# A fused language-model block: in SyncE's list of DMA work of a step, the two stack loads are moved to the end

## Chip, cores, metric

One core of one Trainium2 chip. The metric is the device time of one execution in microseconds (us), median of several runs. The program is given each engine's instructions in a fixed order, written out by hand; engines meet at semaphores alone.

## What is computed

For 32 sequences of 512 tokens, width 128: an embedding of position, nesting depth and segment times a matrix; attention with 8 heads of 16 channels on its layernorm; and a gated mixture of 4 low-rank experts on the layernorm of that. Each adds to its input.

```python
h = tok(x, pos_table, nest_table, seg_table, W)                     # [32, 512, 128]
h = h + attn(layernorm(h), qkv_w, qkv_b, out_w, out_b)
h = h + ffn(layernorm(h), gate_w, thr_w, fc1_w, lora_A, lora_B, fc2_w)

# attn: 8 heads of c = 16
scores = einsum('bshc,bthc->bhst', q, k) / sqrt(c)
ctx = einsum('bhst,bthc->bshc', softmax(scores), v)
out = ctx @ out_w.T + out_b

# ffn: weights = relu(softmax(xf @ gate_w.T) - sigmoid(xf @ thr_w.T) / 4), made to sum to 1
lo = relu(xf @ fc1_w[e].T) @ lora_A[e] @ lora_B[e] @ fc2_w[e].T     # for each expert e
out = sum over e of weights[:, e] * lo
```

## The kernel before

The work is a software pipeline over sequences. Step t (t = -4 to 34) does parts of up to nine sequences at once: it embeds sequence t + 4, makes q, k and v of t + 3, the row maxima of t + 2 and t + 1, the softmax products of t, and projection and experts of t - 2 and t - 3. A step has 16 slots. In each slot TensorE (PE) runs two tiles of scores for row maxima (L642, "mix<-kstk,qstk"), two tiles of the scores that go into the exponential (L621, "sc<-qstk,kstk"), one product of another part, and in every second slot the product with the values (L632, "pv"). VectorE (DVE) takes the row maxima (L876), ScalarE (ACT) the exponentials (L504).

Queries and keys are split in three bf16 pieces each. The pieces are stored to DRAM ("stack_dram<-pieces", L308, six DMAs a sequence) and loaded back, replicated and rearranged, as 96 partitions of `qstk` and `kstk` (three DMAs each, L315 and L322; 1.5 MB a sequence). These are the stack loads, `("stack", 3, 0)` and `("stack", 3, 1)`: in step t they are those of sequence t + 3, and four buffers of them exist. The first reader is L642 of that sequence, in slot 8 of step t + 1.

The softmax subtracts the row maximum inside the matmul: 24 further partitions of `qstk` hold the maxima of each row, turned by PE (product "mT", slot 12), copied by ACT into `mT` (L531) and spread by one DMA of 192 KB, `("max_in", 1, 0)`, "qstk<-mT" (L338). In step t it is that of sequence t + 1, and the first L621 of step t + 1 waits for it (`s_mrow`). Half 0 of sequence t's denominators is stored just ahead of it (`("den_out", 0, 0)`, L328, after ACT's copy of slot 12); behind it the gate weights of sequence t - 2 are stored (`weights_out`, L334, after ACT's copy of slot 12) and loaded back as rows (`weights_in`, "wrow<-w_dram", L366), which first waits until the store has landed. `weights_in` is read by DVE (L950) in slot 3 of the next step.

All these DMAs are issued by SyncE (SP) on one queue, in the order of the list `SP_WORK`: each entry is a kind of work, the sequence relative to t, and a part. SP runs the list once a step; where an entry waits, all behind it wait. Behind the list's end stands the next step's beginning: the token rows ("ids_b", needed by DVE in slot 9), the first piece (which waits for ACT's piece, and for the q stack of the sequence before it to have landed, since the DRAM buffer is single: `upto(sp, s_stk[side], b - 1, 48)`), half 1 of the denominators (`den_out`, L328), two more pieces, and the load of the denominators (`den_in`, L344, after both halves have landed), which DVE inverts in slot 7 (L895).

Of the kernel before, what the change touches and what calls it, by code (L numbers as in the profile page):

```python
# [76 lines left out]
SP_WORK = [  # L77
    ("ids", 4, 0), ("piece", 3, (0, 0)), ("den_out", -1, 1), ("piece", 3, (0, 1)), ("piece", 3, (0, 2)),
    ("den_in", -1, 0), ("piece", 3, (1, 0)), ("piece", 3, (1, 1)), ("out", -3, 0), ("piece", 3, (1, 2)),
    ("rden_out", -1, 0), ("rden_in", -1, 0), ("stack", 3, 0), ("stack", 3, 1), ("den_out", 0, 0), ("max_in", 1, 0),  # L80
    ("weights_out", -2, 0), ("weights_in", -2, 0),
]

EPS = 1e-5
# [962 lines left out]
```

## Time and profile before

| | |
|---|---|
| median of 3 runs | 1260.97 us (1260.73 to 1262.85) |
| the profiled execution | 1249.84 us, span of its instructions 1248.0 us |
| PE busy | 1140.1 us, 91% of the span |
| DVE, ACT, GpSimd (POOL) busy | 908.2, 821.6, 592.6 us |
| mean granted clock of PE | 0.963 of full speed |
| moved by DMA | 123.98 MB, 99 GB/s over the span |

The busy time of PE is modelled at its ends: a matmul of 512 columns is shown 0.38 us long, but the next may start 0.22 us after it. Full steps run from about 190 to 1116 us of the span; ahead of them the pipeline fills, behind them it drains.

### The profile page before, as it was taken

The page shows a single profiled execution, that of the slowest core. Times are in us where ns is not written, and L with a number is a line of the kernel's source. Part 1 is how long each engine was busy: PE and PEld are TensorE (multiplying, and loading weights), DVE is VectorE, ACT ScalarE, POOL GpSimd, SP SyncE. Part 2 cuts the span into 40 slices and gives each one's busy share as a digit, 9 for nine tenths or more (in the row PEclk, how much of TensorE's full clock was granted, in tenths as well). Part 3 has the DMA queues.
Part 4 walks back from the last instruction along what each step waited for, and adds up shares of the span by engine and source line. Part 5 has one row for each costly group of instructions (what it writes and reads, how often), then busy time and mean ns, then how long its engine had stood idle before and what let it go on. Part 6 is the DMA issues. An engine that isn't in the chain of part 4 may idle for free.

```text
span 1248.0 us, 20409 instructions
## 1 busy us (share of the span) xinstructions
PE 1140.1 (91%) x6392; PEld 447.1 (36%) x6392; DVE 908.2 (73%) x2370; ACT 821.6 (66%) x1602; POOL 592.6 (47%) x588
## 2 busy tenths in 40 slices
PE   3579799999999999999999999999999999999985
PEld 1223333333333333333434333333333333333332
DVE  6387687777787877777778777777788777778422
ACT  0217677777777766767777777767777777677851
POOL 2643454455445545544455445544554555432222
PEclk7669999999999999999999999999999999999988
DMA  3654444344455543445544434445544444451111
GB/s 81 140 103 87 104 98 101 92 102 102 111 117 114 114 99 95 100 95 113 121 110 113 99 94 106 103 109 117 113 116 104 99 92 108 102 114 43 44 62 35
DMA packets 88377, 123.98 MB, mean 99 GB/s; under 512 B 17469, under 2 KB 69054, under 8 KB 82054
## 3 DMA queue, kind: packets, MB, share of 16 engines
q1 hardware_dynamic: 86720, 121.08, 42.8%
q10 hardware_dynamic: 1550, 1.59, 0.5%
q8 instruction: 52, 0.85, 0.3%
q14 instruction: 55, 0.45, 0.1%
HBM read 80.81 MB, written 34.95 MB: 93 GB/s over the span
## 4 chain that ended last, share of the span: by engine, by line
PE 65%; DMA 23%; DVE 5%; ACT 2%; issue 2%; POOL 2%; SPq 0%; POOLq 0%; ACTq 0%; DVEq 0%
DMA qstk<-mT 20%; PE pv L632 15%; PE mix L642 14%; PE sc L621 14%; PE mix L659 4%; PE mix L664 3%; PE mix L654 3%; PE mix L694 2%; PE mix L710 2%; PE mix L677 2%; DVE negmax L876 2%; PE mix L699 2%; ACT mT L531 1%; PE mix L684 1%; DMA wrow<-w_dram 1%
## 5 line engine op out<-in xcount | busy, mean ns | idle before, releaser
L876 DVE TENSOR_REDUCE negmax<-mix 128x1 f32<-128x512 f32 x1024 | 672.9, 682 | 176.6 <-PE mix L642 172.4
L504 ACT ACTIVATE probs<-sc 128x512 f32<-128x512 f32 x1024 | 583.7, 598 | 239.6 <-PE sc L621 235.4
L621 PE MATMUL sc<-qstk,kstk 120*128 120x512 bf16 x1024 | 383.6, 384 | 39.1 <-DMA qstk<-mT 38.5
L642 PE MATMUL mix<-kstk,qstk 96*128 96x512 bf16 x1024 | 355.8, 390 | 11.2 <-DVE negmax L876 5.6
L632 PE MATMUL pv<-probs,vals 128*32 128x512 f32 x2048 | 272.7, 604 | 0.0
L457 POOL TENSOR_TENSOR ctxh<-ctx_sb,rdenb 128x512 f32<-128x512 f32 x64 | 81.3, 1270 | 304.0 <-DMA rdenb<-rden_dram 303.8
L642 PEld LDWEIGHTS mix<-kstk,qstk 96*128 96x128 bf16 x1024 | 99.8, 98 | 334.2 <-DVE negmax L876 198.0
L621 PEld LDWEIGHTS sc<-qstk,kstk 120*128 120x128 bf16 x1024 | 99.2, 97 | 175.8 <-issue 57.2
L694 PE MATMUL mix<-xn2T,fc1T_sb 128*128 128x512 f32 x256 | 134.5, 609 | 0.0
L413 POOL TENSOR_TENSOR hb_sb<-h_sb,obias 128x512 f32<-128x512 f32 x32 | 40.7, 1271 | 140.9 <-DVE h L901 140.9
L562 ACT ACTIVATE hid<-mix 128x512 f32<-128x512 f32 x128 | 76.5, 598 | 26.9 <-PE mix L694 26.9
L424 POOL TENSOR_TENSOR pieces<-qk,pieces 128x512 bf16<-128x512 f32 x64 | 74.2, 1160 | 36.5 <-ACT pieces L519 36.4
L901 DVE TENSOR_TENSOR h<-mix,hb_sb 128x512 f32<-128x512 f32 x32 | 22.1, 692 | 85.2 <-PE mix L677 85.2
L441 POOL TENSOR_TENSOR pieces<-qkr,pieces 128x512 bf16<-128x512 f32 x64 | 74.0, 1157 | 8.5
L632 PEld LDWEIGHTS pv<-probs,vals 128*32 128x32 f32 x2048 | 40.4, 108 | 102.7 <-issue 75.8
L418 POOL TENSOR_TENSOR qkr<-qk,pieces 128x512 f32<-128x512 f32 x64 | 74.1, 1158 | 0.0
L406 POOL TENSOR_TENSOR ve<-mv,eps_sb 128x4 f32<-128x4 f32 x64 | 13.0, 203 | 126.8 <-DVE mv L872 126.8
L659 PE MATMUL mix<-xnT,qkvT_sb 128*128 128x512 f32 x128 | 70.4, 636 | 1.6 <-ACT xnT L509 1.4
L408 POOL TENSOR_TENSOR rstd<-ve,minus_half 128x4 f32<-128x4 f32 x64 | 65.2, 1019 | 5.0
L654 PE MATMUL mix<-id,xn 128*128 128x128 f32 x256 | 41.8, 289 | 23.4 <-POOL xn L450 15.2
L537 ACT COPY ctx_sb<-pv 128x512 f32<-128x512 f32 x64 | 37.6, 588 | 36.0 <-PE pv L632 36.0
L694 PEld LDWEIGHTS mix<-xn2T,fc1T_sb 128*128 128x128 f32 x256 | 49.6, 196 | 21.9 <-issue 4.6
(116 smaller groups left out, 1066.9 us busy)
## 6 DMA issues: line engine op xcount, KB each, us to landing
stack_dram<-pieces SPq DMA_DIRECT2D x192, 128.0 KB
rdenb<-rden_dram SPq DMA_DIRECT2D x64, 256.0 KB
qstk<-stack_dram SPq DMA_DIRECT2D x32, 384.0 KB, 6.4
kstk<-stack_dram SPq DMA_DIRECT2D x32, 384.0 KB, 8.7
qstk<-stack_dram SPq DMA_DIRECT2D x32, 256.0 KB, 6.8
kstk<-stack_dram SPq DMA_DIRECT2D x32, 256.0 KB, 9.4
wrow<-w_dram SPq DMA_DIRECT2D x32, 256.0 KB
out<-out_sb SPq DMA_DIRECT2D x32, 256.0 KB, 2.3
```

Of the source, the lines that this page charges most:

```text
L418: pool.tensor_tensor(qkr[:, side, :], qk32[:, side, :], pieces[:, side, 0, :], ALU.subtract).then_inc(s_res0, 1)
L424: pool.tensor_tensor(pieces[:, side, 1, :], qk32[:, side, :], pieces[:, side, 0, :], ALU.subtract).then_inc(s_pc1, 1)
L457: pool.tensor_tensor(ctxh[:, g, :], ctx_sb[:, u % 2, g, :], rdenb[:, g, :], ALU.mult).then_inc(s_ctxh, 1)
L504: act.activation(probs[:, c % 8, i % 2], sc[:, i % RING], ACT.Exp).then_inc(s_exp, 1)
L562: act.activation(hid[:, e, :], aux(f"fc1_{e}", 1), ACT.Relu).then_inc(s_hid, 1)
L621: pe.matmul(sc[:, i % RING, :], kstk[0:KROWS, u, h, j * P:(j + 1) * P], qstk[0:KROWS, u, h, :], start=True, stop=True).then_inc(s_score, 1)
L632: mm = pe.matmul(pv[Q * i:Q * i + Q, :], vals[:, u, 2 * half + jj, 4 * g + i, :], probs[:, 4 * (r % 2) + i, jj, :], start=(half == 0 and j ...
L642: pe.matmul(max_bank(m), qstk[0:STK, u, h, j * P:(j + 1) * P], kstk[0:STK, u, h, :], start=True, stop=True).then_inc(s_mxmm, 1)
L654: mm = pe.transpose(aux(name)[:, j, :], src[:, j, :], id32[:])
L659: pe.matmul(aux("qk"[side], 1), qkvT_sb[:, side, :], xnT[:], start=True, stop=True).then_inc((s_qmm, s_kmm)[side], 1)
L694: pe.matmul(aux(f"fc1_{e}", 1), fc1T_sb[:, e, :], xn2T[:], start=True, stop=True).then_inc(s_fc1mm, 1)
L876: dve.tensor_reduce(negmax[:, m // NT, m % NT:m % NT + 1], max_bank(m), AX.X, ALU.max, negate=True).then_inc(s_max, 1)
```

## The change

```diff
@@ -77,8 +77,8 @@
 SP_WORK = [
     ("ids", 4, 0), ("piece", 3, (0, 0)), ("den_out", -1, 1), ("piece", 3, (0, 1)), ("piece", 3, (0, 2)),
     ("den_in", -1, 0), ("piece", 3, (1, 0)), ("piece", 3, (1, 1)), ("out", -3, 0), ("piece", 3, (1, 2)),
-    ("rden_out", -1, 0), ("rden_in", -1, 0), ("stack", 3, 0), ("stack", 3, 1), ("den_out", 0, 0), ("max_in", 1, 0),
-    ("weights_out", -2, 0), ("weights_in", -2, 0),
+    ("rden_out", -1, 0), ("rden_in", -1, 0), ("den_out", 0, 0), ("max_in", 1, 0), ("weights_out", -2, 0),
+    ("weights_in", -2, 0), ("stack", 3, 0), ("stack", 3, 1),
 ]
```

No other engine's order changes, and no instruction is added or taken away. In SP's order, this is a full step from the load of the inverted denominators ("rdenb") to the next step's first piece, before:

```order
L359 DMA rdenb<-rden_dram 128x1x512 x2
L315 DMA qstk<-stack_dram 48x1x4096
L315 DMA qstk<-stack_dram 32x1x4096
L315 DMA qstk<-stack_dram 16x4096
L322 DMA kstk<-stack_dram 48x4096
L322 DMA kstk<-stack_dram 32x1x4096
L322 DMA kstk<-stack_dram 16x4096
L328 DMA den_dram<-ctx_sb 4x512
L338 DMA qstk<-mT 24x8x512
L334 DMA w_dram<-wT 4x4x128
L366 DMA wrow<-w_dram 128x1x512
L301 DMA ids_b<-ids_dram 64x512
```

The same place in the changed kernel:

```order
L359 DMA rdenb<-rden_dram 128x1x512 x2
L328 DMA den_dram<-ctx_sb 4x512
L338 DMA qstk<-mT 24x8x512
L334 DMA w_dram<-wT 4x4x128
L366 DMA wrow<-w_dram 128x1x512
L315 DMA qstk<-stack_dram 48x1x4096
L315 DMA qstk<-stack_dram 32x1x4096
L315 DMA qstk<-stack_dram 16x4096
L322 DMA kstk<-stack_dram 48x4096
L322 DMA kstk<-stack_dram 32x1x4096
L322 DMA kstk<-stack_dram 16x4096
L301 DMA ids_b<-ids_dram 64x512
```

The six stack loads have moved past four DMAs and past the waits of three of them: for ACT's copies of slot 12 and for the landing of the weights' store. They now stand directly ahead of the next step's token rows.

## Rows read from the trace of the kernel before

**Rows 1.** The page's shares, by line, of the chain that ended last

```profile
DMA qstk<-mT 20%; PE pv L632 15%; PE mix L642 14%; PE sc L621 14%; PE mix L659 4%; PE mix L664 3%; PE mix L654 3%; PE mix L694 2%; PE mix L710 2%; PE mix L677 2%; DVE negmax L876 2%; PE mix L699 2%; ACT mT L531 1%; PE mix L684 1%; DMA wrow<-w_dram 1%
```

**Rows 2.** Waits of the whole span: who for whom, us, times, longest

```profile
PE sc L621 <- DMA qstk<-mT: 38.5, 30, 5.5
...
PE mix L642 <- DVE negmax L876: 5.6, 11, 1.4
```

**Rows 3.** PE in time: start, us, line, [idle before <- releaser]

```profile
578.61 0.39 PE L642 MATMUL mix<-kstk,qstk 96*128 96x512 bf16 x1
578.84 0.38 PE L621 MATMUL sc<-qstk,kstk 120*128 120x512 bf16 x1
...
583.17 0.39 PE L642 MATMUL mix<-kstk,qstk 96*128 96x512 bf16 x1
584.68 0.39 PE L621 MATMUL sc<-qstk,kstk 120*128 120x512 bf16 x1 [1.12 <-DMA qstk<-mT]
...
601.90 0.39 PE L642 MATMUL mix<-kstk,qstk 96*128 96x512 bf16 x1
```

**Rows 4.** PE in time, the first L621 of three other full steps

```profile
439.65 0.39 PE L621 MATMUL sc<-qstk,kstk 120*128 120x512 bf16 x1 [2.51 <-DMA qstk<-mT]
...
475.56 0.39 PE L621 MATMUL sc<-qstk,kstk 120*128 120x512 bf16 x1 [1.53 <-DMA qstk<-mT]
...
619.46 0.39 PE L621 MATMUL sc<-qstk,kstk 120*128 120x512 bf16 x1 [0.40 <-DMA qstk<-mT]
```

**Rows 5.** PE in time, first L621 of two steps, 0.61 us instead of 0.39

```profile
153.58 0.61 PE L621 MATMUL sc<-qstk,kstk 120*128 120x512 bf16 x1 [5.51 <-DMA qstk<-mT]
...
547.80 0.61 PE L621 MATMUL sc<-qstk,kstk 120*128 120x512 bf16 x1 [2.37 <-DMA qstk<-mT]
```

**Rows 6.** Stretches: us, busy of PE, PEld, DVE, ACT, POOL; clock, DMA share, GB/s

```profile
153.50:159.50 6.00, 5.92 (x27) 3.73 (x27) 3.40 (x10) 2.88 (x5) 1.27 (x1) 0.61 0.00 0
547.50:552.50 5.00, 4.70 (x23) 3.23 (x27) 2.25 (x5) 2.32 (x5) 1.27 (x1) 0.68 0.22 72
```

**Rows 7.** SP's issues in time, one full step: start, us of issuing, DMAs

```profile
569.86 1.85 SPq L315 DMA_DIRECT2D qstk<-stack_dram  x3
571.80 1.57 SPq L322 DMA_DIRECT2D kstk<-stack_dram  x3
...
576.18 0.89 SPq L338 DMA_DIRECT2D qstk<-mT  x1
577.17 0.63 SPq L334 DMA_DIRECT2D w_dram<-wT  x1
584.87 0.55 SPq L366 DMA_DIRECT2D wrow<-w_dram  x1
...
591.51 0.62 SPq L308 DMA_DIRECT2D stack_dram<-pieces  x1
594.19 0.53 SPq L328 DMA_DIRECT2D den_dram<-ctx_sb  x1
...
597.37 0.40 SPq L344 DMA_DIRECT2D den<-den_dram  x1
```

**Rows 8.** SP's issues in time in a step of the draining end

```profile
1139.91 0.84 SPq L338 DMA_DIRECT2D qstk<-mT  x1
1140.85 0.64 SPq L334 DMA_DIRECT2D w_dram<-wT  x1
1143.56 0.54 SPq L366 DMA_DIRECT2D wrow<-w_dram  x1
```

**Rows 9.** Stretches of that step: us; clock, DMA share, GB/s

```profile
1141.00:1143.50 2.50, 1.00 0.39 92
1143.50:1144.50 1.00, 1.00 0.00 0
```

**Rows 10.** DMA issues: KB each, median us from issue to landing

```profile
qstk<-stack_dram SPq DMA_DIRECT2D x32, 128.0 KB, 8.5
kstk<-stack_dram SPq DMA_DIRECT2D x32, 128.0 KB, 10.8
```

**Rows 11.** DVE in time, same step as rows 7

```profile
601.05 0.34 DVE L895 RECIPROCAL rden<-den 128x32 f32<-128x32 f32 x1
```

**Rows 12.** The loads of the denominators, min/median/max of issue to landing

```profile
DMA to landing us min/median/max: 1.6/2.1/3.1
```

## The prediction

> **What bounds the kernel now.** I read the chain of waits first. The reader is to see that one DMA, the spreading of the turned maxima, is 20% of the chain that ended last, and that everything else of size in it is PE's own matmuls [rows 1]. The list of waits gives the same from PE's side: the first L621 of a step waits for that DMA, 38.5 us in 30 steps, while PE lost only 5.6 us to VectorE's row maxima, most of it while the pipeline fills [rows 2]. PE in time shows where it stands: L642 starts at 583.17, and the L621 behind it only at 584.68, with 1.12 us of idle time before it [rows 3].
>
> Is PE the bound outside this wait? Compare the distance between first L621s with the wait in it. From 439.65 to 475.56 it is 35.91 us, with 1.53 us idle at its end; from 584.68 to 619.46 it is 34.78 us with 0.40 us idle [rows 3, 4]. To the idle time I add 0.16 us, since it is counted from the modelled end of L642 (583.17 + 0.39), while an L621 behind L642 otherwise starts 0.23 us after its start (578.61 and 578.84) [rows 3]: the step truly lost 584.68 - 583.17 - 0.23 = 1.28 us, not 1.12. Then both distances without their waits are 34.22 us. A long wait gives the other engines nothing that makes the rest of the step shorter, and a short one takes nothing from them. So no other engine stands close behind, and a step without the wait should take 34.22 us.
>
> **Why the maxima come late.** SP issues the six stack loads at 569.86 to 573.4, then, when ACT has copied, the maxima at 576.18 and the weights' store at 577.17 [rows 7]. The last part of the k stack lands a median 10.8 us after its issue [rows 10], so at about 572.8 + 10.8 = 583.6. The maxima, behind them on the same queue, let PE go at 584.68, 8.5 us after their issue. The end of the program shows the same DMA with no stack load ahead of it, since there no sequence t + 3 exists: issued at 1139.91, and the core's DMA engines are empty from 1143.5 on [rows 8, 9], so at most 3.6 us. That tail is this change's steady state for this DMA, seen in the kernel before.
>
> By the Trainium skill (DMA: Bandwidth & Descriptors, Queues, rings and completion order) descriptors on each DMA engine are consumed in ring order. The trace agrees: 8.5 us behind the stacks against at most 3.6 us without them. The page's fit for a single DMA (Anatomy of one DMA, for the GpSimd path), 2.0 us + bytes / 436e3, would give 192 KB an estimated 2.5 us; either value clears the need below, so the sum is the same by both.
>
> **The change, part by part.** *Maxima:* issued at 576.18 as before (ACT's copy ends then, and SP was already free), landed by 576.18 + 3.6 = 579.8. PE wants them at 583.17 + 0.23 = 583.4. Cover 3.6 us, so the wait goes whole, also where the maxima were longest under way. Saved: 38.5 us, and 30 x 0.16 = 4.8 us of hidden ends; 43.3 us.
>
> *Clock:* behind two of the waits, 5.51 and 2.37 us long, PE ran at half its clock (1.2 instead of 2.4 GHz): the L621 there takes 0.61 us [rows 5]. Granted clock 0.61 over 6.0 us costs (1 - 0.61) x 6.0 = 2.3 us, and 0.68 over 5.0 us costs 1.6 us, of which 0.2 us lies in the wait itself [rows 6]; I take 2.3 + 1.4 = 3.7 us. The wait of 2.51 us at 439.65 had no such cost [rows 4]. Without the waits the two should be gone.
>
> *Weights' store and rows:* at the end of the program the rows' load follows its store by 2.7 us, in a full step now by 7.7 us [rows 7, 8]. So it is issued at about 579.9, five us earlier than now, and nobody waits for it: gain and cost nothing.
>
> *Stack loads:* they follow the rows' load, at 580.4 to 584.0. SP stood idle in just that time, waiting for the weights' store, and the token rows behind them were issued at 585.4 anyway: no entry of the next step is issued later. What is late is the landing. By [rows 10], counted from the issue of each: last q part 581.7 + 8.5 = 590.2, last k part 583.5 + 10.8 = 594.3. These durations had 512 KB of "rdenb" ahead of them and the maxima beside them; now 256 KB of weights' rows, so they are rather an upper bound; the lower bound is some 9 us from 580.4, 589.5.
>
> Who needs them, in a timeline in which the next step begins 1.3 us sooner? (a) The first L642 of that sequence, 601.90 - 1.3 = 600.6 [rows 3]: 6.3 us of cover against 18 now. (b) The next first piece, 591.51 - 1.3 = 590.2 [rows 7], waits for the q stack: cover nothing or 0.5 us. Were it 1 us late, SP would still be free ahead of the denominators' store at 594.19 - 1.3 = 592.9. (c) That store and the pieces are now queued behind the end of the k stack; this is the narrow place. The load of the denominators is due at 597.37 - 1.3 = 596.1 and lands 2.1 us later [rows 7, 12], at 598.2; VectorE inverts at 601.05 - 1.3 = 599.8 [rows 11]. With a stack that lands at 594.3, the store behind it lands at about 595, ahead of 596.1. Cost nothing; cover 1.1 us there and 1.6 us behind it.
>
> *Filling:* the same holds in the first steps. The wait of 5.51 us at 153.58 is one where rdenb, stacks and maxima were all issued directly behind one another; it goes too, and is in the 38.5.
>
> **Sum.** 38.5 + 4.8 + 3.7 = 47.0 us. The profiled execution would go from 1249.84 to 1202.8 us (span 1248.0 to 1201). The shown median is 11.1 us above the profiled execution. I take this as an offset that stays: 1260.97 - 47.0 = 1214.0 us.
>
> **Rivals.**
>
> *More is won (0.15).* If the 11.1 us are longer waits for the same DMA, or more half-clock stretches (8 of 1.4 us would make them), they go too, and the time is near 1203 us. For it: the waits scatter from 0.40 to 2.51 us [rows 4]. Against: nothing in one profile shows what the other runs did.
>
> *Part is won (0.13).* The wait goes, and another takes part of its place: the denominators' chain by under 1 us a step, or VectorE, busiest in slots 8 to 12, now that PE never pauses. Half the gain left would be 1237 us. Against: the constant 34.22 us.
>
> *Slower (0.07).* The denominators' store waits behind the stacks. If the stacks land at L, the store lands at about L + 0.8 and the denominators at L + 2.9; VectorE's inversion, and with it its row maxima and PE, wait from L = 596.9 on. At L = 598.3 the wait equals the 1.44 us that a step won (1.28 and its share of the rest), and from there the kernel is slower: at L = 599, 0.7 us in each of 28 steps, 1281 us. It needs stack loads that take 5 us longer than their 10.8 us.
> By the Trainium skill's rule of ring order (same page and section) the store indeed has to pass behind the stacks on its DMA engines, which is what speaks against the change. No row before shows it, as the queue was empty then.
>
> *The change does nothing (0.03).* The maxima would have to be held by ACT's copy and not the queue; the tail rows speak against it. 1261 us.
>
> **How the numbers follow.** My forecast, 1214 us, has 0.62 with its own range 1206 to 1222. The range of 8 in 10 takes in most of the larger gain and the nearer half of the partial one: 1200 to 1229. A measurement of this kernel tells about 0.2%, 2.5 us, from no change. Faster is 0.62 + 0.15 + 0.13 = 0.90; of the rest 0.03 are the same and 0.07 slower.
>
> **What would show it.** Right: the wait of L621 for "qstk<-mT" is gone from the list of waits, and the DMA from the chain; first L621s are 34.2 us apart; the rows' load follows its store by some 2.7 us; stack loads are issued directly behind it; granted clock 1.00 throughout the full steps. Wrong: a wait of VectorE's inversion (L895) for "den<-den_dram", a wait of L642 in slot 8 for the stacks, or SP waiting for the q stack ahead of the first piece for over 2 us. What makes the prediction wrong is above all the landing time of the stacks beside the weights' rows, which no row before shows.

## The result, and the profile after

| | before | changed |
|---|---|---|
| median | 1260.85 us (4 runs, 1258.06 to 1262.85) | 1203.22 us (4 runs, 1201.68 to 1204.20) |
| ratio, 95% interval | | 0.9543 (0.9522 to 0.9564) |
| profiled execution, span | 1249.84 us, 1248.0 us | 1203.50 us, 1201.7 us |

The changed kernel is 57.6 us faster by its medians and 46.3 us by the two profiled executions. One execution among those of the experiments, the profiled one of e4, took 2223.3 us, with a matmul of L621's kind at 664 ns instead of 382 on average and a recorded clock of 1.00; nothing on record explains it, and the medians below leave it out. The page of the changed kernel gives, of its shares, the line of the engines, that of the chain by line, and that of L621 (busy, mean ns, then idle before it):

```profile
PE 1129.4 (94%) x6392; PEld 443.3 (37%) x6392; DVE 909.0 (76%) x2370; ACT 820.8 (68%) x1602; POOL 592.9 (49%) x588
...
PE pv L632 19%; PE mix L642 18%; PE sc L621 17%; PE mix L694 8%; PE mix L659 4%; PE mix L710 3%; PE mix L664 3%; PE mix L699 2%; PE mix L677 2%; PE mix L654 2%; DVE negmax L876 1%; PE mix L684 1%; DMA wrow<-w_dram 1%; PE mix L648 1%; PE mix L670 0%
...
L621 PE MATMUL sc<-qstk,kstk 120*128 120x512 bf16 x1024 | 382.2, 382 | 0.6 <-ACT probs L504 0.3
```

"DMA qstk<-mT", 20% of the chain before [rows 1], is gone from it, and L621's idle time with it: 0.6 us, where it waited 38.5 us for the maxima alone [rows 2].

PE in time, at the beginnings of two steps next to one another:

```profile
555.37 0.38 PE L621 MATMUL sc<-qstk,kstk 120*128 120x512 bf16 x1
555.59 1.05 PE L677 MATMUL mix<-wo_q_sb,ctxn 128*128 128x128 f32 x8
...
589.35 0.39 PE L642 MATMUL mix<-kstk,qstk 96*128 96x512 bf16 x1
589.58 0.38 PE L621 MATMUL sc<-qstk,kstk 120*128 120x512 bf16 x1
589.79 1.05 PE L677 MATMUL mix<-wo_q_sb,ctxn 128*128 128x128 f32 x8
```

L621 now starts 0.23 us behind L642 (1.51 us before, [rows 3]), and the steps are 589.58 - 555.37 = 34.21 us apart.

SP's issues in the same step:

```profile
582.35 0.87 SPq L338 DMA_DIRECT2D qstk<-mT  x1
583.33 0.65 SPq L334 DMA_DIRECT2D w_dram<-wT  x1
585.78 0.54 SPq L366 DMA_DIRECT2D wrow<-w_dram  x1
586.41 1.86 SPq L315 DMA_DIRECT2D qstk<-stack_dram  x3
588.37 1.57 SPq L322 DMA_DIRECT2D kstk<-stack_dram  x3
...
597.63 0.66 SPq L308 DMA_DIRECT2D stack_dram<-pieces  x1
599.07 0.54 SPq L328 DMA_DIRECT2D den_dram<-ctx_sb  x1
...
602.25 0.40 SPq L344 DMA_DIRECT2D den<-den_dram  x1
```

The rows' load follows its store by 2.45 us instead of 7.7 [rows 7], and the stacks are issued into the time that SP used to spend waiting there. VectorE inverts the denominators where it did, relative to the step, without a gap:

```profile
605.93 0.34 DVE L895 RECIPROCAL rden<-den 128x32 f32<-128x32 f32 x1
```

From its issue, the last part of the q stack now takes 0.8 us longer to land and that of the k stack as long as before ([rows 10]: 8.5 and 10.8 us). The token rows behind them land later too (3.9 and 4.4 us before), and nobody waits for them:

```profile
qstk<-stack_dram SPq DMA_DIRECT2D x32, 128.0 KB, 9.3
kstk<-stack_dram SPq DMA_DIRECT2D x32, 128.0 KB, 10.7
ids_b<-ids_dram SPq DMA_DIRECT2D x32, 64.0 KB, 8.7
ids_b<-ids_dram SPq DMA_DIRECT2D x32, 32.0 KB, 9.9
```

Two of SP's own waits (us in total, times, longest) show where its time went; both are entered under L269, the helper that waits. The first was short before (8.2 us in 3 times); the wait for the weights' store was 184.4 us in 31 times.

```profile
SPq L269 <- DMA qstk<-stack_dram: 169.3, 31, 7.1
...
SPq L269 <- DMA w_dram<-wT: 54.5, 31, 3.6
```

### The profile page after: what moved, and what is told of

It reads as the page before. It is cut to its first block, busy times and chain, and to the rows that moved or that the text cites. A ratio compares the mean times of both kernels' runs of the same rounds, so it can differ in the third digit from the quotient of the medians.

```text
span 1201.7 us, 20409 instructions
## 1 busy us (share of the span) xinstructions
PE 1129.4 (94%) x6392; PEld 443.3 (37%) x6392; DVE 909.0 (76%) x2370; ACT 820.8 (68%) x1602; POOL 592.9 (49%) x588
## 3 DMA queue, kind: packets, MB, share of 16 engines
q1 hardware_dynamic: 86720, 121.08, 43.3%
## 4 chain that ended last, share of the span: by engine, by line
PE 80%; DVE 3%; DMA 2%; POOL 1%; issue 1%; ACT 0%; SPq 0%; POOLq 0%; DVEq 0%; ACTq 0%
PE pv L632 19%; PE mix L642 18%; PE sc L621 17%; PE mix L694 8%; PE mix L659 4%; PE mix L710 3%; PE mix L664 3%; PE mix L699 2%; PE mix L677 2%; PE mix L654 2%; DVE negmax L876 1%; PE mix L684 1%; DMA wrow<-w_dram 1%; PE mix L648 1%; PE mix L670 0%
## 5 line engine op out<-in xcount | busy, mean ns | idle before, releaser
L621 PE MATMUL sc<-qstk,kstk 120*128 120x512 bf16 x1024 | 382.2, 382 | 0.6 <-ACT probs L504 0.3
L642 PE MATMUL mix<-kstk,qstk 96*128 96x512 bf16 x1024 | 355.1, 389 | 11.3 <-DVE negmax L876 5.1
L642 PEld LDWEIGHTS mix<-kstk,qstk 96*128 96x128 bf16 x1024 | 99.5, 98 | 333.2 <-DVE negmax L876 197.6
L621 PEld LDWEIGHTS sc<-qstk,kstk 120*128 120x128 bf16 x1024 | 99.2, 97 | 128.3 <-issue 57.0
```

The costliest lines, as they stand in the source:

```text
L621: pe.matmul(sc[:, i % RING, :], kstk[0:KROWS, u, h, j * P:(j + 1) * P], qstk[0:KROWS, u, h, :], start=True, stop=True).then_inc(s_score, 1)
L642: pe.matmul(max_bank(m), qstk[0:STK, u, h, j * P:(j + 1) * P], kstk[0:STK, u, h, :], start=True, stop=True).then_inc(s_mxmm, 1)
```

## Experiments

Each set ran on one chip, with the kernel before beside it: 1252.4 us (29 runs, 1243.2 to 1261.8) in the first (e0 to e3), 1246.2 us (7 runs, 1237.6 to 1251.6) in the second (c0, e4 to e6), 1257.2 us (7 runs, 1249.7 to 1261.1) in the third (e8, e9). Ratios are to that kernel on that chip, with 95% intervals.

| label | what | median us | ratio |
|---|---|---|---|
| e0_before_again | the kernel before | 1253.3 | 1.0006 (0.9977 to 1.0036) |
| e1_stacks_before_weights | stacks behind the maxima, ahead of the weights | 1261.8 | 1.0095 (1.0059 to 1.0130) |
| e2_only_k_last | only the k stack moved | 1204.8 | 0.9619 (0.9580 to 0.9659) |
| e3_max_on_act_queue | order of before, maxima on ScalarE's queue | 1252.0 | 1.0006 (0.9971 to 1.0041) |
| c0_changed_again | the changed kernel | 1202.9 | 0.9654 (0.9597 to 0.9711) |
| e4_512k_ahead_of_stacks | changed, + 512 KB ahead of the stacks | 1203.5 | 0.9652 (0.9595 to 0.9710) |
| e5_1280k_ahead_of_stacks | changed, + 1280 KB ahead of the stacks | 1225.4 | 0.9825 (0.9775 to 0.9876) |
| e6_1536k_ahead_of_maxima | changed, + 1536 KB ahead of the maxima | 1206.8 | 0.9680 (0.9632 to 0.9728) |
| e8_3072k_ahead_of_maxima | changed, + 3072 KB ahead of the maxima | 1374.8 | 1.0945 (1.0889 to 1.1002) |
| e9_512k_again | e4 again | 1202.1 | 0.9568 (0.9514 to 0.9622) |

### e0_before_again and c0_changed_again: where the 11 us went

Both kernels unchanged.

> The kernel before, unchanged, to see what its other executions do with the 11 us by which its median stood above its profiled execution (1249.8 us). Theory A (more half-clock stretches): the mean granted clock of the longer executions is lower, by about 0.009 for 11 us (11 us of 1250 at half clock cost 11 us more and lower the mean by 11 / 1260), so 0.954 beside 0.963, at times near 1260 us. Theory B (longer waits for the maxima, clock unchanged): spans near 1259 us at a mean clock of 0.963, and in a profile of such an execution an L621 wait for the maxima of 1.3 + 11 / 30 = 1.65 us a step. Theory C (a fixed offset outside the span): spans stay at 1248 us while times are 1260 us.

> The changed kernel, unchanged, beside the dose kernels. If the scatter of the kernel before (19 us over 29 runs) is that of its waits for the maxima, this kernel, which has none, stays within some 4 us: 1201 to 1205 us. If the scatter is one of the chip, it shows the same 15 to 19 us.

The kernel before scatters over 11 to 19 us on each of the three chips, the changed one over 1.9 us (1202.4 to 1204.2) here and over 2.5 us in the result above. So the scatter belongs to what the change removed. Theory C falls: the profiled execution of e0 took 1252.6 us with a span of 1250.8, the usual 1.8 us outside. Between A and B, this one profile speaks for A. Its waits for the maxima are shorter than those of [rows 2] (35.7 us in 26 recorded times), yet it is 2.8 us longer; stretches of 15 us (length, busy of PE, PEld, DVE, ACT, POOL, clock, DMA share, GB/s) show more places below full clock than the two behind [rows 5]:

```profile
140.00:155.00 15.00, 10.42 (x58) 4.40 (x51) 8.43 (x22) 6.38 (x13) 6.61 (x8) 0.79 0.66 117
155.00:170.00 15.00, 15.00 (x86) 5.38 (x85) 11.88 (x30) 11.91 (x24) 11.04 (x11) 0.98 0.18 49
185.00:200.00 15.00, 12.38 (x66) 4.89 (x59) 8.64 (x21) 7.50 (x14) 6.80 (x8) 0.89 0.19 46
545.00:560.00 15.00, 12.73 (x65) 5.47 (x62) 8.30 (x20) 7.30 (x14) 7.94 (x9) 0.89 0.15 42
575.00:590.00 15.00, 13.20 (x64) 6.09 (x62) 8.93 (x24) 8.74 (x18) 6.96 (x7) 0.89 0.65 116
830.00:845.00 15.00, 13.13 (x68) 5.02 (x67) 9.02 (x21) 8.25 (x15) 6.96 (x8) 0.89 0.21 48
```

(1 - clock) x 15 us summed over these is 3.15 + 0.3 + 4 x 1.65 = 10.1 us; the same sum in the first profile is 5.1 us (stretches of 0.88, 0.89 and 0.89). The sums count some of the waiting itself, at a low clock, so they are upper bounds of the cost; their difference, 5.0 us, less 2.8 us of shorter waits, is 2.2 of the 2.8 us. In the changed kernel no stretch between 110 and 1130 us is below full clock:

```profile
110.00:1090.00 980.00, 977.03 (x5683) 382.23 (x5682) 797.29 (x2077) 733.58 (x1432) 517.04 (x504) 1.00 0.48 110
```

No execution of about 1260 us was itself profiled, but the mean granted clock of all 41 executions of this kernel on this chip is on record. The ten longest average 1258.9 us at a clock of 0.958, the ten shortest 1247.2 us at 0.965. By theory A's own working (0.009 for 11 us) the 11.7 us between them would go with 0.0096; it is 0.0065. So half-clock stretches make, by this estimate, about two thirds of the excess, and the rest would be longer waits, as theory B has it: one execution of 1260.0 us had a clock of 0.965. It is a rough estimate, since the mean takes in filling and draining, where the clock varies in the changed kernel too (means of 0.962 to 0.973 at nearly the same time).

The kernel before also differs from chip to chip: its medians are 1246.2, 1252.4 and 1257.2 us at median clocks of 0.961 to 0.962, and 1260.9 us in the result, while the changed kernel's are 1202.9 and 1203.2 us. What is won is therefore 43.3 us on the second set's chip and 57.6 us in the result. No run shows what differs between the chips, and the record does not name the chip of the first profile.

### e1_stacks_before_weights: is the place of the maxima all?

```diff
-    ("rden_out", -1, 0), ("rden_in", -1, 0), ("stack", 3, 0), ("stack", 3, 1), ("den_out", 0, 0), ("max_in", 1, 0),
+    ("rden_out", -1, 0), ("rden_in", -1, 0), ("den_out", 0, 0), ("max_in", 1, 0), ("stack", 3, 0), ("stack", 3, 1),
     ("weights_out", -2, 0), ("weights_in", -2, 0),
```

> Only the half-0 denominators' store and the maxima are moved ahead of the stack loads; the weights' store and rows stay behind them. Theory (one queue in ring order, each DMA lands behind what is ahead of it): the wait for the maxima is gone as in the changed kernel, but the weights' store is issued at 580.8 behind the stacks, lands near 590.5, the rows near 593.5, and VectorE wants them in slot 3 at 590.7: 2.8 us of wait in each full step, so about 1203 + 28 x 2.8 = 1280 us, slower than before. Rival (only the place of the maxima counts): 1203 us, no wait for the rows.

The wait for the maxima is gone, and the gain is lost whole: 1261.8 us. SP issues the rows' load 8.3 us behind the weights' store, because the store now stands behind the stacks, and VectorE's product (L950) is the next one late. The trace gives its releaser as "issue"; the load's issue at 583.17 puts it there.

```profile
574.86 0.69 SPq L334 DMA_DIRECT2D w_dram<-wT  x1
583.17 0.56 SPq L366 DMA_DIRECT2D wrow<-w_dram  x1
```

```profile
588.45 0.69 DVE L950 TENSOR_TENSOR low<-mix,wrow 128x512 f32<-128x512 f32 x1 [3.80 <-issue]
```

```profile
577.69 1.05 PE L677 MATMUL mix<-wo_q_sb,ctxn 128*128 128x128 f32 x8
...
613.82 1.05 PE L677 MATMUL mix<-wo_q_sb,ctxn 128*128 128x128 f32 x8
```

The steps are 36.13 us apart, 1.9 us over 34.2. VectorE waited 3.8 us where I had expected 2.8, but PE lost only half of that, having other work until its L642 had to wait for that product:

```profile
PE mix L642 <- DVE low L950: 31.1, 27, 2.2
```

The rival falls: the weights' store has to stand ahead of the stacks as well.

### e2_only_k_last: half of the bytes

```diff
-    ("rden_out", -1, 0), ("rden_in", -1, 0), ("stack", 3, 0), ("stack", 3, 1), ("den_out", 0, 0), ("max_in", 1, 0),
-    ("weights_out", -2, 0), ("weights_in", -2, 0),
+    ("rden_out", -1, 0), ("rden_in", -1, 0), ("stack", 3, 0), ("den_out", 0, 0), ("max_in", 1, 0), ("weights_out", -2, 0),
+    ("weights_in", -2, 0), ("stack", 3, 1),
```

> Only the k stack load moves to the end; the q stack load stays ahead of the maxima. Theory (what counts is how many bytes are ahead of the maxima): 768 KB less ahead of them, 8.5 us become at most 8.5 - 768 KB / 190 GB/s = 4.4 us, under the 7.2 us that they may take, so no wait: 1203 us, as the changed kernel. Rival (any load ahead on the queue makes the maxima late, or the k stack alone behind the rows does no good): a wait of half the size stays, about 1230 us.

1204.8 us, as the theory had it. One wait for the maxima is left in the whole program, where the pipeline fills; it has the size of the 1.6 to 1.9 us by which this kernel is behind the two medians of the changed one:

```profile
148.96 0.39 PE L621 MATMUL sc<-qstk,kstk 120*128 120x512 bf16 x1 [1.90 <-DMA qstk<-mT]
```

### e3_max_on_act_queue: is it the queue?

```diff
-    ("rden_out", -1, 0), ("rden_in", -1, 0), ("stack", 3, 0), ("stack", 3, 1), ("den_out", 0, 0), ("max_in", 1, 0),
+    ("rden_out", -1, 0), ("rden_in", -1, 0), ("stack", 3, 0), ("stack", 3, 1), ("den_out", 0, 0),
...
                 act.copy(mT[:], aux("mT", 1)[0:3 * NH]).then_inc(s_mT, 1)
+                upto(act, s_mT, b)
+                act.dma_start(qstk[STK:KROWS, u, :, :],
+                              mT[:].unsqueeze(1).broadcast_to([3 * NH, NH, S])).then_inc(s_mrow, 16)
```

> SP's order as before, with the stack loads early, but the maxima are issued by ScalarE on its own queue, directly behind its copy. Theory (the maxima stood in line behind the stacks on SP's queue): on another queue they land in 3.6 to 5 us although the stacks are still under way, the wait of L621 is gone and the time is near 1203 us, up to 10 us more where ScalarE, full in slots 12 and 13, loses 0.9 us a step to issuing. Rival (the DMA engines' bandwidth is what is short, whichever queue): they land as late as before, 8 us, and the time stays near 1250 to 1261 us.

My theory fell, as I had put it: 1252.0 us, no gain. The maxima had a queue to themselves and nothing ahead of them on it, and a DMA of them took 8.37 us in the chain of this kernel:

```profile
610.87 8.37 DMA qstk<-mT
```

The single records of the DMA packets, grouped by me, say why. Maxima are packets of 1 KB (192 in each load), stacks packets of 8 KB (192 in each step). Times are us of the span, each for one load of a full step; the last column counts the 8 KB packets that started from the issue on.

```
kernel    maxima on      issued   first 1 KB packet   last 1 KB packet   landed   8 KB packets from issue on
before    SP's queue     611.68   614.84              618.73             619.42   96 (last at 617.66)
e3        ACT's queue    610.87   614.59              618.21             619.24   93 (last at 615.76)
changed   SP's queue     582.35   583.87              585.19             585.60    0
```

Over all 32 loads, the median from issue to landing is 8.4 us before, 8.5 us in e3 and 3.2 us in the changed kernel. On either queue the maxima's packets start over 3 us after the issue, instead of 1.5, and are then spread over nearly 4 us instead of 1.3. About half of the stacks' packets are still to be moved when the maxima are issued, and the DMA engines get through them first for the most part. By the Trainium skill (DMA: Bandwidth & Descriptors, Queues, rings and completion order) each DMA engine goes round between the queues that have work, packet by packet; the late start on ScalarE's queue shows that this did not let the small load past here. ScalarE also paid: its issuing takes 0.82 us in its busiest slot, and PE waits for its copy behind that. Both waits are in the list:

```profile
PE sc L624 <- DMA qstk<-mT: 20.8, 19, 6.1
...
PE mix L645 <- ACT wT L560: 14.2, 28, 0.5
```

### e6 and e8: something else ahead of the maxima

```diff
-    ("rden_out", -1, 0), ("rden_in", -1, 0), ("den_out", 0, 0), ("max_in", 1, 0), ("weights_out", -2, 0),
+    ("rden_out", -1, 0), ("rden_in", -1, 0), ("extra", 0, 0), ("den_out", 0, 0), ("max_in", 1, 0), ("weights_out", -2, 0),
...
+            def load_extra(b):
+                upto(sp, s_extra, b - 1, 16)
+                sp.dma_start(extra_dram, posT.unsqueeze(1).broadcast_to([P, 6, S])).then_inc(s_extra, 16)
```

In e8 the 6 is a 12. The copy goes to a scratch tensor that nobody reads.

> The changed kernel with one more copy of 1536 KB, DRAM to DRAM, where the stack loads stood before: behind the inverted denominators' rows, ahead of the half-0 denominators and the maxima. The stacks stay at the end. Theory (bytes ahead of the maxima make them late, whatever they are): the wait for qstk<-mT is back, 0.5 to 2.5 us a step, 1240 to 1265 us. Rival (it is the stack loads themselves, their many writes to the same SBUF partitions as the maxima): a copy that does not touch SBUF leaves the maxima in time, 1203 us.

> As e6, with 3072 KB. In e6 the DMA engines moved the copy at 217 to 391 GB/s and were done with it and the maxima by about 586, 3 us after the maxima's issue at 583.06; the stack loads had moved at 190. So the 1536 KB there did not occupy the engines until the maxima's issue plus their cover. Theory (what counts is how long the engines are busy with what is ahead, on the queue, of the maxima): 3072 KB keep them busy some 5 us longer, to 590, the maxima land near 592, 1.7 us or more after PE wants them: the wait for qstk<-mT is back in nearly every step and the time is 1250 us or more. Rival (only writes into the same SBUF rows delay the maxima): no such wait, at most 1215 us.

The same number of bytes as the stacks does nothing much, against the theory: e6 takes 1206.8 us, and its list has two short waits for the maxima (us in total, times, longest).

```profile
PE sc L629 <- DMA qstk<-mT: 1.8, 2, 1.4
```

The maxima are late there too, but within their cover: 4.1 us from issue to landing by the median, against 3.2. So bytes alone are the wrong measure. When the maxima were issued, at 583.06, the copy had at most 296 of its 768 packets of 2 KB to go, and the last of them started 2.7 us later; behind the issue of the maxima in the kernel before, the last of the stacks' packets started 6.0 us later. The stretches of e6 show how soon the DMA engines were free (length, clock, DMA share, GB/s):

```profile
580.00:582.00 2.00, 1.00 0.85 257
582.00:584.00 2.00, 1.00 1.03 391
584.00:586.00 2.00, 1.00 0.63 204
586.00:588.00 2.00, 1.00 0.04 13
```

Twice as much brings the wait back, larger than it ever was, though nothing of it touches the maxima's rows of SBUF:

```profile
PE sc L629 <- DMA qstk<-mT: 108.9, 31, 8.7
```

The maxima, issued at 659.14 in one step of e8, found the DMA engines busy for some 7 us more:

```profile
660.00:662.00 2.00, 1.00 1.04 391
662.00:664.00 2.00, 1.00 1.05 368
664.00:666.00 2.00, 1.00 0.97 348
666.00:668.00 2.00, 1.00 0.38 144
```

e8 is 117.6 us slower than the kernel before on its chip (1257.2 us), with a mean granted clock of 0.922. With the median of 10.4 us from issue to landing that settles it against the rival: what delays the maxima is that the DMA engines are still busy with what was issued ahead of them, whatever it is.

### e4, e5 and e9: how much cover the stacks have at their new place

```diff
-    ("weights_in", -2, 0), ("stack", 3, 0), ("stack", 3, 1),
+    ("weights_in", -2, 0), ("extra", 0, 0), ("stack", 3, 0), ("stack", 3, 1),
```

with the same copy, of 512 KB (e4, e9) or 1280 KB (e5). In the first text, 294.3 and 296.9 are the 594.3 and 596.9 of the prediction.

> The changed kernel with one more copy of 512 KB, DRAM to DRAM, in each step from 0 on, between the weights' rows and the stack loads. It tells how much cover the stacks have at their new place. By the prediction's sum they may land 2.6 us later (L from 294.3 to 296.9 in units of that step) before VectorE's inversion waits; 512 KB at 190 GB/s are 2.8 us. So 1203 to 1210 us, with an L895 wait for the denominators of under 0.5 us a step. Rival (there is no such narrow place, cover until the first L642 in slot 8, 6.3 us): exactly 1203 us, no L895 wait.

> As the last, with 1280 KB: 6.9 us at 190 GB/s, 4.3 us over the cover. Theory (the denominators' chain is the narrow place): L895 waits for den<-den_dram, up to 4 us in each of 31 steps, 1203 + 31 x 4 = about 1320 us, slower than the kernel before. Rival (cover is 6.3 us, at L642 in slot 8): about 1203 + 31 x 0.6 = 1222 us, with waits of L642 and none of L895.

> e4 again, for a profile of an undisturbed execution: 1203.5 us as before. The last k part lands 10.7 us after its issue or later by up to 1.5 us, L895 waits in no or few steps, and SP waits for the landing of the half-1 denominators longer than the changed kernel's 4.6 us in all.

512 KB cost nothing (1203.5 and 1202.1 us). In e9 the inversion waits once, 0.4 us, and SP waits 6.9 us in 8 times for the half-1 denominators' store, against 4.6 us in 4 times in the changed kernel, as expected. 1280 KB cost 22 us. The last k part was issued later and took 13.1 us instead of 10.7; from the issue of the weights' rows to its landing it is about 17.9 us instead of 14.3, so 3.6 us later, not the 6.9 that I had counted. What then waits is the chain that the prediction named: SP for the half-1 denominators' store to land, VectorE's inversion, and PE for VectorE's row maxima behind it (L672 here, L664 in the changed kernel, where it is 2.8 us in 4 times).

```profile
SPq L346 <- DMA den_dram<-ctx_sb: 62.2, 31, 4.7
```

```profile
DVE rden L903 <- DMA den<-den_dram: 20.4, 26, 1.7
...
PE mix L672 <- DVE negmax L884: 21.2, 28, 2.0
```

3.6 us later less the cover of 2.6 us leaves 1.0 us; the inversion waits 0.8 us each time. The time, 1225.4 us, is close to the rival's 1222 and far from the theory's 1320, but that is chance: the rival's waits of L642 (here L650) for the stacks do not appear, beyond one of 2.7 us in the filling that the kernel before has too (3.3 us). The theory had the right wait and too large a size for it.

## Why the prediction was right or wrong

**The bound.** Right. The two distances without their waits gave 34.22 us; the changed kernel's steps are 34.21 us apart, in the step shown and by the median of all full steps. No other engine had stood close behind.

**Maxima and clock.** Right in the profile: 47.0 us forecast for the profiled execution, 46.3 us measured, 1201 us forecast for the span, 1201.7 measured. The wait is gone in all 30 steps, and so is every half-clock stretch of the full steps. The tail of the program foretold the new landing: at most 3.6 us there; in the changed kernel it takes 3.2 to 3.5 us in all 32 loads. The prediction's second value for it, 2.5 us, was too short, and changed nothing in the sum.

**The offset.** Wrong, and this is the whole distance between 1214.0 and 1203.2 us, which also lies below the forecast's own range of 1206 to 1222. The step was "I take this as an offset that stays". The 11.1 us by which the median stood above the profiled execution went too, as the first rival had it, at 1203 us; I had given that 0.15. One profile is one draw from a kernel whose executions differ by up to 19 us, and I had no ground to treat the rest as fixed. Half-clock stretches and longer waits both seem to be in it (e0), and perhaps a difference between chips; how much of each is open, but all of it went with the wait.

**The cause of the lateness.** Half right. I put it as a matter of one queue's order. e3 shows that another queue does not help, e6 and e8 that occupied DMA engines are what counts. The prediction's two times, 8.5 us behind the stacks and at most 3.6 us without, fit either account. The sum did not depend on it.

**Weights' store and rows.** Right that the rows' load comes earlier, 2.45 us behind its store, and that nobody waits for it in the full steps. The prediction gave this part neither gain nor cost; e1 shows that it decides: with the stacks between maxima and weights, the move would have cost 1% instead of winning 4%.

**Stacks.** Right in place and time. Shifting the forecast by 6.18 us (first L621 at 583.4 there, at 589.58 in the profile) the half-1 store was due at 599.08 and came at 599.07, the denominators' load at 602.28 and came at 602.25, the inversion at 605.98 and came at 605.93. The first piece was forecast with a cover of nothing or 0.5 us; it is 1.2 us late (597.63 against 596.4), behind the q stack, whose last part takes 9.3 us and not 8.5. SP was still free before the store, as worked out. One sign that the prediction gave for being wrong did appear by its letter: SP waited for the q stack ahead of the first piece for more than 2 us, 169.3 us in 31 times. It was a bad sign to name, since it takes SP's idle time for lateness. Before, SP stood idle there all the same, for ACT's pieces:

```profile
SPq L308 <- ACT pieces L519: 186.4, 32, 14.0
```

In the changed kernel that wait is 28.5 us in 6 times.

**The rivals.** The slower one had the right place and a fair cover (e4, e5), but its price assumed stacks 5 us later, which nothing made so. The partial one and "no change" did not occur.

## What to carry to other kernels

A small DMA that an engine waits for should be issued when the DMA engines are empty, or nearly so: behind a bulk load it is late by what the engines still have to move, on a queue of its own as well (e3), and it does harm once that exceeds its cover (e6, e8). Bulk loads with many microseconds of slack go behind the small ones, into a time in which the issuing engine would wait anyway; but look for every small transfer in that stretch, since leaving one behind the bulk only moves the wait (e1). A draining end, where some of the transfers no longer exist, can show in the trace of before what the change will do, as it did here. And where executions scatter, ask whether it is the wait to be removed that scatters, before a difference between median and profile is carried over as fixed.

## What was not expected of the hardware

A load of 192 KB with a queue to itself took 8.5 us beside a bulk load on the other queue, as on the same one (8.4 us), and 3.2 us with the engines empty. While the stacks moved, a stretch of 8 us showed 199 GB/s in the kernel before and 178 GB/s in the changed one; stretches of 2 us with a DRAM-to-DRAM copy of 2 KB rows showed up to 391 GB/s. PE fell to half its clock after a wait of 1.8 us in one execution (585.65 us of e0's profile, L621 of 0.61 us), while one of 2.51 us in another had no such cost [rows 4].
